# A GRU's candidate rows get a PSUM bank of their own, and the table stage keeps the transposed embedding

## The reference

```python
x = emb_table[input_ids]                       # (2048, 50, 128), a table of 12,501 rows
def step(h, xt):                               # 50 steps, h is (2048, 128)
    rec = h @ rec_kernel + b_r
    xz, xr, xh = jnp.split(xt, 3, axis=-1)
    rz, rr, rh = jnp.split(rec, 3, axis=-1)
    z = jax.nn.sigmoid(xz + rz)
    r = jax.nn.sigmoid(xr + rr)
    hh = jnp.tanh(xh + r * rh)
    return z * h + (1.0 - z) * hh
...
logits = last @ emb_table.T                    # (2048, 12501), fp32
```

## Time and profile before

| | |
|---|---|
| median of 3 runs | 1371.12 us (1370.25 to 1375.16) |
| the profiled execution's own time | 1370.22 us |
| its span, from the first to the last instruction | 1368.1 us |
| mean granted TensorE clock | 0.933 of 2.4 GHz |
| PE busy | 1180.8 us (86%) |
| PE's weight loads | 795.3 us (58%) |
| POOL busy | 784.2 us (57%) |
| DVE busy | 692.4 us (51%) |
| ACT busy | 686.6 us (50%) |
| DMA engines, mean | 215 GB/s |

### The profile page before, as it was taken

How to read it: one execution, slowest core, us unless ns; L and a number is a source line. 1 busy time by engine, 2 the same in 40 slices (tenths; PEclk the granted TensorE clock), 3 DMA queues, 4 the chain that set the end, 5 groups by cost and what they waited for, 6 DMA issues and landing times.

```text
span 1368.1 us, 16235 instructions
## 1 busy us (share of the span) xinstructions
PE 1180.8 (86%) x5590; PEld 795.3 (58%) x5590; DVE 692.4 (51%) x1191; ACT 686.6 (50%) x1203; POOL 784.2 (57%) x812
## 2 busy tenths in 40 slices
PE   7947778777878778778799999999999999999998
PEld 7933444343444334444466666666666668888776
DVE  7624455444545445445554555545555555444554
ACT  3522333333433333333456666666666667777644
POOL 0027667666776767667666666666666655555200
PEclk9979898888988888989999999999999999999999
DMA  8965555555555555555467887777887778888799
GB/s 292 366 179 153 142 152 146 147 152 141 154 146 148 146 154 146 148 143 159 132 196 239 260 254 253 250 238 253 256 261 253 237 249 269 285 282 284 239 365 333
DMA packets 127489, 294.21 MB, mean 215 GB/s; under 512 B 18096, under 2 KB 33456, under 8 KB 127408
## 3 DMA queue, kind: packets, MB, share of 16 engines
q0 software_dynamic: 51200, 157.34, 39.3%
q1 hardware_dynamic: 76208, 135.84, 29.6%
HBM read 171.30 MB, written 121.81 MB: 214 GB/s over the span
## 4 chain that ended last, share of the span: by engine, by line
PE 67%; another core or an unknown queue 11%; DVE 6%; ACT 6%; issue 5%; DMA 4%; POOL 0%; SPq 0%; DVEq 0%; ACTq 0%; POOLq 0%
PE r_ps L406 12%; PE c_ps L406 11%; PE z_ps L406 10%; PE x_ps L457 6%; PE x_ps L459 5%; PE x_ps L458 5%; PE c_ps L399 5%; PE r_ps L399 4%; PE z_ps L399 3%; DVE c_ps L765 2%; DMA gate_table<-gates 2%; ACT gates L562 2%; ACT gates L564 1%; DMA out_dram<-logits 1%
## 5 line engine op out<-in xcount | busy, mean ns | idle before, releaser
L335 POOL DMA_INDIRECT gathered<-gate_table,index x800 | 782.3, 978 | 495.9 <-issue 204.1
L564 ACT ACTIVATE gates<-z_ps,zr_bias 128x512 f32<-128x512 f32 (+1 forms) x250 | 151.6, 607 | 329.7 <-PE z_ps L406 162.7
L768 DVE TENSOR_TENSOR kept<-gates,state 128x512 f32<-128x512 f32 (+1 forms) x250 | 147.2, 589 | 237.5 <-ACT gates L564 192.0
L406 PE MATMUL r_ps<-state,w_rec_sb 128*128 128x512 f32 (+1 forms) x500 | 256.6, 598 | 0.0
L772 DVE SCALAR_TENSOR_TENSOR gates<-gates 128x512 f32<-128x512 f32 (+1 forms) x250 | 146.1, 585 | 209.0 <-issue 125.4
L399 PE MATMUL c_ps<-ident,gathered 128*128 128x128 f32 x800 | 116.4, 260 | 145.7 <-DVE c_ps L765 125.2
L406 PE MATMUL c_ps<-state,w_rec_sb 128*128 128x512 f32 (+1 forms) x500 | 235.1, 554 | 0.0
L406 PE MATMUL z_ps<-state,w_rec_sb 128*128 128x512 f32 (+1 forms) x500 | 233.8, 550 | 0.0
L399 PEld LDWEIGHTS c_ps<-ident,gathered 128*128 128x128 f32 x800 | 92.0, 144 | 232.6 <-DVE c_ps L765 180.7
L765 DVE SCALAR_TENSOR_TENSOR c_ps<-c_ps,bias_sb,gates 128x512 f32<-128x512 f32 (+1 forms) x250 | 162.0, 648 | 126.2 <-PE c_ps L406 47.2
L562 ACT ACTIVATE gates<-r_ps,zr_bias 128x512 f32<-128x512 f32 (+1 forms) x250 | 151.0, 604 | 143.3 <-PE r_ps L406 56.6
(11 more groups left out here) (78 smaller groups left out, 870.8 us busy)
## 6 DMA issues: line engine op xcount, KB each, us to landing
out_dram<-logits SPq DMA_DIRECT2D x192, 512.0 KB, 4.7
gate_table<-gates SPq DMA_DIRECT2D x24, 768.0 KB, 4.1
gathered<-gate_table,index POOLq DMA_INDIRECT x800
emb_rows<-in_L_rec_emb_table_dram SPq DMA_DIRECT2D x48, 256.0 KB, 4.6
out_dram<-logits SPq DMA_DIRECT2D x8, 213.0 KB, 3.9
logits<-in_r_input_ids_dram SPq DMA_DIRECT2D x1, 400.0 KB, 6.1
logits<-in_r_input_mask_dram SPq DMA_DIRECT2D x1, 400.0 KB, 6.5
gate_table<-gates SPq DMA_DIRECT2D x2, 192.0 KB, 9.2
```

Source lines behind the costliest of these rows:

```text
L335: nc.gpsimd.indirect_dma_start(gathered[:, q, n, :].bitcast(F32), None, table, bass.IndirectOffsetOnAxis(ap=index[:, g, n:n + 1], axis=0)) ...
L406: return nc.tensor.matmul(bank, w_rec_sb[:, gate * H:(gate + 1) * H], h, start=first, stop=True, skip_group_check=True)
L564: nc.scalar.activation(z_sb[:, b, 0:width], z_ps[:, b, 0:width], ACT.Sigmoid, bias=zr_bias[:, 0:1]).then_inc(s_z, 1)
```

## The change

Three things are changed together.

The candidate rows are turned into a bank pair of their own (x_ps), right behind the r rows. The state's candidate part stays alone in c_ps; DVE scales it into SBUF and adds the turned rows in a further instruction; ACT takes the tanh from SBUF. To make room, c_ps and z_ps have one bank each in place of two, and the logit units have a pair named u_ps. PE's matmul into c_ps now waits for the scaling of the block before, its z rows for the z sigmoid of the block before, its candidate rows for the addition two blocks before. A gather waits for `s_z_in` of the block four before.

`meanwhile` is now called ahead of the state's r matmul, behind both row groups, and `after` is gone: both logit units of a block stand there, whatever its width, and ACT copies both between its z sigmoid and its tanh.

The table stage splits the transposed chunks straight into embT_hi and embT_lo, which the logits use later, and the first stage's loads, transposes and copies of the vocabulary are gone. For this, `table_chunk` now gives partition p the rows p, 128 + p, 256 + p and 384 + p of a chunk. The projections use r_ps and x_ps in place of z_ps and r_ps; the last stage uses u_ps and r_ps.

```diff
-        z_sb, r_sb, cand = gates[:, 0], gates[:, 1], gates[:, 2]
+        z_sb, r_sb, pre = gates[:, 0], gates[:, 1], gates[:, 2]
-        rowsT_hi = state_hi[:, 2:4]
-        rowsT_lo = state_lo[:, 2:4]
...
-        z_ps = psum("z_ps", [P, SETS, BANK])
         r_ps = psum("r_ps", [P, SETS, BANK])
-        c_ps = psum("c_ps", [P, SETS, BANK])
-        x_ps = psum("x_ps", [P, 2, CHUNK])
+        x_ps = psum("x_ps", [P, SETS, BANK])
+        c_ps = psum("c_ps", [P, BANK])
+        z_ps = psum("z_ps", [P, BANK])
+        u_ps = psum("u_ps", [P, 2, CHUNK])
...
-            return rows[bass.ds(chunk * CHUNK, CHUNK), :].rearrange("(p n) h -> p n h", n=TPC)
+            return rows[bass.ds(chunk * CHUNK, CHUNK), :].rearrange("(n p) h -> p n h", p=P)
...
-            sp.wait_ge(s_rowsT_ps, FULL + 1)
-            for j, m in RAGGED:
-                sp.dma_start(emb_rows[0:m, 0, j, :], emb[ragged_rows(j, m), :]).then_inc(s_rows, 16)
-            for k in range(1, K2 - 1):
-                sp.wait_ge(s_rowsT, k)
-                sp.dma_start(emb_rows[:, 0], emb_chunk(k - 1)).then_inc(s_rows, 16)
...
-                    pool.wait_ge(s_turned, (k - 1) * QS + q + 1)
+                    pool.wait_ge(s_z_in, (k - 1) * QS + q + 1)
...
                 pe.wait_ge(s_gather[q], done)
-                pe.wait_ge(s_z, g + 1)
                 add_rows(r_bank, blk, q, 1, True)
+                if g >= SETS:
+                    pe.wait_ge(s_sum, g + 1 - SETS)
+                add_rows(x_bank, blk, q, 2, True)
+                if meanwhile is not None:
+                    meanwhile()
                 if started is not None:
                     pe.wait_ge(s_start, started)
                 if not start:
                     pe.wait_ge(s_state, g + 1 - SETS)
-                add_state(r_bank, h, 1, False).then_inc(s_rec, 1)
-                add_state(c_bank, h, 2, True).then_inc(s_rec, 1)
+                add_state(r_bank, h, 1, False).then_inc(s_r_in, 1)
+                if g > 0:
+                    pe.wait_ge(s_scaled, g)
+                add_state(c_bank, h, 2, True).then_inc(s_c_in, 1)
+                pe.wait_ge(s_z, g + SETS)
                 add_rows(z_bank, blk, q, 0, True)
                 add_state(z_bank, h, 0, False).then_inc(s_z_in, 1)
-                if meanwhile is not None:
-                    meanwhile()
-                pe.wait_ge(s_scaled, g + 1)
-                add_rows(c_bank, blk, q, 2, False).then_inc(s_turned, 1)
-                if after is not None:
-                    after()
...
-                if tiles_of(blk) == TPL:
-                    return (lambda: work((0,)), lambda: work((1,)))
-                return (lambda: work((0, 1)), None)
+                return lambda: work((0, 1))
...
-                act.wait_ge(s_rec, 2 * g + 1)
+                act.wait_ge(s_r_in, g + 1)
                 nc.scalar.activation(r_sb[:, b, 0:width], r_ps[:, b, 0:width], ACT.Sigmoid, bias=zr_bias[:, 1:2]).then_inc(s_r, 1)
                 act.wait_ge(s_z_in, g + 1)
-                nc.scalar.activation(z_sb[:, b, 0:width], z_ps[:, b, 0:width], ACT.Sigmoid, bias=zr_bias[:, 0:1]).then_inc(s_z, 1)
+                nc.scalar.activation(z_sb[:, b, 0:width], z_ps[:, 0:width], ACT.Sigmoid, bias=zr_bias[:, 0:1]).then_inc(s_z, 1)
                 if meanwhile is not None:
                     meanwhile()
-                act.wait_ge(s_turned, g + 1)
-                nc.scalar.activation(cand[:, b, 0:width], c_ps[:, b, 0:width], ACT.Tanh, bias=bias_sb[:, 0, 2:3]).then_inc(s_cand, 1)
-                if after is not None:
-                    after()
+                act.wait_ge(s_sum, g + 1)
+                nc.scalar.activation(pre[:, b, 0:width], pre[:, b, 0:width], ACT.Tanh, bias=bias_sb[:, 0, 2:3]).then_inc(s_cand, 1)
...
-                return (None, work) if tiles_of(blk) == TPL else (work, None)
+                return work
...
-                dve.wait_ge(s_rec, 2 * g + 2)
+                dve.wait_ge(s_c_in, g + 1)
                 dve.wait_ge(s_r, g + 1)
-                nc.vector.scalar_tensor_tensor(out=c_bank, in0=c_bank, scalar=bias_sb[:, 1, 2:3], in1=r,
+                nc.vector.scalar_tensor_tensor(out=new, in0=c_ps[:, 0:width], scalar=bias_sb[:, 1, 2:3], in1=r,
                                                op0=ALU.add, op1=ALU.mult).then_inc(s_scaled, 1)
+                dve.wait_ge(s_scaled, g + 1)
+                nc.vector.tensor_tensor(new, new, x, ALU.add).then_inc(s_sum, 1)
                 dve.wait_ge(s_z, g + 1 + SETS)
                 nc.vector.tensor_tensor(kept_b, z, h, ALU.mult).then_inc(s_kept, 1)
```

More of the change, by code:

```diff
@@ L181, in gru_logits @@
         s_scaled = sem("s_scaled")
+        s_sum = sem("s_sum")
         s_cand = sem("s_cand")
@@ L348, in turn_rows @@
                 for j, m in tiles:
-                    turned = nc.tensor.transpose(x_ps[:, bank, j * P:j * P + m], emb_rows[0:m, slot, j, :],
+                    turned = nc.tensor.transpose(u_ps[:, bank, j * P:j * P + m], emb_rows[0:m, slot, j, :],
                                                  ident[0:m, 0:m].bitcast(F32))
@@ L358, in transpose_rows, with project @@
                 turn_rows(s % 2, s, tiles).then_inc(s_rowsT_ps, 1)
-            def project(c, k, tiles=WHOLE, first=False):
+            def project(c, tiles=WHOLE, first=False):
                 pe.wait_ge(s_rowsT_lo, c + 1)
@@ L365, in project @@
                         pe.wait_ge((s_proj_dve, s_proj_act)[j % 2], c * (TPC // 2) + j // 2 - 1)
-                    bank = (z_ps, r_ps)[j // 2][0:m, j % 2, 0:G]
-                    high = rowsT_hi[:, k, j * P:j * P + m]
-                    low = rowsT_lo[:, k, j * P:j * P + m]
+                    bank = (r_ps, x_ps)[j // 2][0:m, j % 2, 0:G]
+                    high = embT_hi[:, c * CHUNK + j * P:c * CHUNK + j * P + m]
+                    low = embT_lo[:, c * CHUNK + j * P:c * CHUNK + j * P + m]
                     nc.tensor.matmul(bank, high, w_in_hi[:], start=True, stop=False)
@@ L375, in _ @@
             pe.wait_ge(s_w_in_parts, 2)
-            project(0, 0, first=True)
+            project(0, first=True)
             for s in range(1, SLOTS):
                 transpose_rows(s + 1, (s + 1) % SLOTS, 1 + (s + 1) // SLOTS)
-                project(s, s % 2)
+                project(s)
             for i in range(1, ROUNDS - 1):
@@ L407, in add_state, with step @@
                                         skip_group_check=True)
-            def step(k, q, blk, done, meanwhile=None, after=None, start=False, started=None):
+            def step(k, q, blk, done, meanwhile=None, start=False, started=None):
                 g = k * QS + q
@@ L414, in step @@
                 h = state[:, lane, c0:c0 + width]
-                z_bank, r_bank, c_bank = (t[:, q % SETS, 0:width] for t in (z_ps, r_ps, c_ps))
+                r_bank, x_bank = r_ps[:, q % SETS, 0:width], x_ps[:, q % SETS, 0:width]
+                c_bank, z_bank = c_ps[:, 0:width], z_ps[:, 0:width]
                 pe.wait_ge(s_gather[q], done)
-                pe.wait_ge(s_z, g + 1)
                 add_rows(r_bank, blk, q, 1, True)
+                if g >= SETS:
[3 more added lines that the diff above has]
+                    meanwhile()
                 if started is not None:
@@ L468, in work @@
                             pe.wait_ge(s_state_lo, parts)
-                        unit(tile + j, None if first else (k - K2) * QS + q, j, v0, width, x_ps[:, j])
-                if tiles_of(blk) == TPL:
-                    return (lambda: work((0,)), lambda: work((1,)))
-                return (lambda: work((0, 1)), None)
+                        unit(tile + j, None if first else (k - K2) * QS + q, j, v0, width, u_ps[:, j])
+                return lambda: work((0, 1))
             for q in range(QS):
-                step(0, q, FIRST[q], landed(0, 0, q), vocabulary(16 * len(RAGGED), None, RAGGED) if q == 0 else None,
-                     start=(q < SETS), started=2)
+                step(0, q, FIRST[q], landed(0, 0, q), start=(q < SETS), started=2)
             for k in range(1, K2):
                 for q in range(QS):
-                    step(k, q, FIRST[q], landed(0, k, q),
-                         vocabulary(16 * k + 16 * len(RAGGED), k, WHOLE) if q == 0 else None)
+                    step(k, q, FIRST[q], landed(0, k, q))
             for q in range(QS):
                 step(K2, q, SECOND[q], landed(K2, K2, q),
-                     *units(K2, q, SECOND[q], q * UPQ, FULL * CHUNK, REST, first=(q == 0), parts=1 + q // 2), started=4)
+                     units(K2, q, SECOND[q], q * UPQ, FULL * CHUNK, REST, first=(q == 0), parts=1 + q // 2), started=4)
             for i in range(1, K3 - K2):
@@ L518, in last_unit, with table_high @@
             tile = 3 * TPL + u % TPL
-            return ((x_ps, z_ps)[u % 4 // 2][:, u % 2], (u + UNITS3) % BUFFERS, nan_row[:, tile:tile + 1])
+            return ((u_ps, r_ps)[u % 4 // 2][:, u % 2], (u + UNITS3) % BUFFERS, nan_row[:, tile:tile + 1])
```

(6 more changed lines are left out.)

106 lines of the change are left out of this document (39 added, 67 removed).

## The result

The changed kernel takes 1498.3 us (median of 4 runs, 1497.2 to 1500.5) beside 1372.0 us before (1370.3 to 1375.2): a ratio of 1.092, 95% interval 1.0895 to 1.0944. The profiled execution has a span of 1496.6 us against 1368.1, 128.5 us more.

A forecast was written before the change was run, and what follows sets the result against it. It took POOL's issue as the first stage's floor and PE as the bound of the second and third; 1370.2 - 34 + 50 + 65 + 6 + 6 gave 1463 us, range 1420 to 1530.

The forecast's parts named there:

- +50: Third stage: logit units waiting for ACT's copies make each of 50 blocks 1.0 us longer, +50 us.
- +65: Second stage: the same wait for copies makes each of 50 block pairs 1.29 us longer, +65 us.
- the loop: Second and third stage: r to z, z sigmoid, first copy, two units, r again; 4.25 us at 256 columns, 5.91 at 512.
- rival 4: Second and third stage: copies are done in time and lengths stay; 1348 us, or 1314 with POOL's floor; chance 0.07.
- The 38 us held back in the second stage: Second stage: z sigmoids of 512 blocks starting late inside the loop, up to +38 us; taken as 0, kept for range.
- rival 3: Second and third stage: clock falls to 1.2 GHz; in half of the blocks +270 us, 1733 us; chance 0.06.
- the middle, -34: First stage: gain from removing PE's wait for scaling before the candidate rows, midway between 0 and -68 us.
- Its own low end: First stage: gain of 0, as late results stay and c and z have one bank each.
- rival 1: Late results don't shrink, so the first stage gains 0, or follow into the loop, second stage +38; 1535 us; chance 0.18.
- POOL's 515 us: First stage: POOL's gather issue sets a floor of about 515 us, 5.15 a block, limiting the gain to 68 us.
- the prediction's 3.4 each: Seams at blocks 100 and 200: units move ahead of r and wait for state_lo, 3.4 us each, +6 together.
- taken as 6, between 3 and 12: Table stage: loads and stores in smaller pieces run slower, +6 us, range 3 to 12.

The follow-up runs named there:

- copies first: Changed kernel with ACT copying a block's two logit units before that block's r sigmoid, not behind its z sigmoid: 1377.3 us, ratio to before 1.003.
- units behind z: Changed kernel with a block's logit units on PE moved behind its z matmul, ACT's order kept: 1367.9 us, one run.
- the table part alone: Kernel before with only the table-stage change: transposed embedding kept, later vocabulary transposes, copies and loads left out: 1375.6 us, ratio 1.0036.
- units behind z at the seams: Copies first, with logit units behind z and their copies behind the z sigmoid at blocks 100 and 200, lane 2's split later: 1384.4 us, ratio 0.9972.
- the kernel with the filler: Copies first, plus an unread 512-column full-precision matmul on PE behind each block 4 to 99: 1287.9 us on the second chip, 1395.3 on the third.

## Why the prediction was right, and where it was off

1. *The copies of the logits: right, term by term.* +50 was +47.9 for 47 blocks, 1.02 us each, and +65 was +63.9 for 48.5 pairs, 1.32 each against 1.29. Of the loop's parts, a sigmoid to the copy behind it took 0.37 (0.36 assumed), the copy to the unit 0.05. Moving the copies alone took 121 of the 126 us away again, and moving the units alone did as much, so rival 4's premise (copies in time) fails for exactly the reason given, ACT's order.
2. *The 38 us held back in the second stage: right to take 0.* In the changed kernel the late r, z and c of blocks 100 to 199 add up to 2.1 us. Before, z alone had 31.9. The prediction's reason (the loop leaves PE idle a fifth of the time) fits the other runs on that chip: with the loop open r, z and c add up to 15.9 us (copies first) and 84.5 us (units behind z) in these blocks. But such a sum is not a cost: the two take 428.5 and 431.5 us for 102 to 199.
3. *The clock: rival 3 didn't come.* With a stand of PE of 0.85 us in each block the granted clock was 0.99 and 1.00 in the two stages, the 2.4 GHz level: gaps of this size, one in 4.26 us, did not take the clock down. The Trainium skill (TensorE: Matmul & The Clock Gate, Why this matters for your kernels) warns of long idle gaps between bursts of matmuls. The trace agrees: around the stand of 6.32 us at the first seam the clock was 0.53 (684 to 695 us).
4. *The first stage: mis-sized, and this is most of the 35 us between 1463 and 1498.* Its step said that between 0 and -68 nothing decides, and took the middle, -34. It measured -2.6 (-9.9 on the third chip). Its own low end had a reason: late results sit on r, z and c alike. They did not shrink (191 us late before, 215 after), and the wait in PE's middle was a place where they were paid, not their source. It moved one matmul on: from 116.5 us ahead of the candidate rows to 79.3 ahead of the next block's c. The first half of rival 1 came true, the second did not. The sum also held POOL's 515 us fixed, and here they were not. POOL's waits did shrink, by 23.5 us in 98 to 681, two thirds of the 34 taken. What took this back is on POOL itself: on the first chip a gather of blocks 4 to 99 takes 1.00 us in the kernel before and in the one with the table part alone, and 1.04 to 1.05 in the three with DVE's addition; on the third chip 0.99 and 1.03 to 1.04. Over the 384 gathers that is 16.4 us on the first chip. The prediction had put DVE's addition at 0 beside POOL; that these 16 us are its price, and not that of another part of the change, isn't shown, and on the second chip kernels with the addition had 0.99 and 1.00. (The prediction's example of 8.6 us between PE and ACT holds other work of ACT until 457.74; ACT stood for 4.2 of them.)
5. *The seams: the unit's move was right, what comes with it was left out.* With the loop open, three blocks over a seam cost 16.3 - 12.9 = 3.4 and 14.8 - 11.4 = 3.4 us, the prediction's 3.4 each. The changed kernel paid +9.2 and +5.9. From the second, two blocks of the loop at 1.0 us take 2.0 and leave 3.9. The first also had r and z of block 99 late by 2.24 and 2.17 us, and a stretch at half clock from 684 to 695 us around the 6.32 us in which PE stood. On the third chip the same three blocks took 26.9 us, so this part moves from run to run.
6. *The table stage: +3.7, taken as 6, between 3 and 12.* Loads and stores in the small pieces do cost something. The hardware queue in 31 to 58 us moved 9.46 MB at a share of 105.3%, 333 GB/s at full share, against 366. That is a tenth less; the piece size of 512 B alone had been worth a fifth. In bytes moved in the same 27 us it is 9.46 against 9.91 MB, 4.5% less, since the share rose. The kernel with the table part alone started block 0 2.7 us later than before. That the piece size makes up all of it isn't shown. The Trainium skill (DMA: Bandwidth & Descriptors, Specifications) gives 512 B as the smallest transfer at line rate, by which the cost would have been 0. The trace disagrees: 333 GB/s against 366.

```profile
q1 hardware_dynamic: 9545, 9.46, 105.3%
```

*What stays open.* Why a result of PE reaches its reader late. PE's ends are modelled in the trace, so it can't even tell whether the matmul ran late or the word of it came late. It is not the gathers alone (the second chip gathers the same rows without it), and not PE's load alone (the first chip without gathers). Nor is PE's pause for a gather needed just before: in the kernel with the units behind z at the seams PE waits for none between blocks 26 and 39, and yet blocks 30 to 32, 37 and 38 have late results. Whether memsets in the gathers' place would bring it on a chip that has it wasn't seen, as that kernel ran on the second chip; nor was the changed kernel timed there. An estimate for that chip: 1496.6 less the 61 us between 575.2 and 513.8 is about 1435 us against the 1290.2 us that the kernel before spanned there, so the verdict would be the same and larger.

## What to carry to other kernels

Where a buffer with one consumer is refilled every round, walk the ring once in the consumer's program order: the copy that frees it, what stands ahead of that copy, and what that waits for. Here the ring closed through the z sigmoid and cost 1.0 us in every block, and moving the copy, not the buffer, opened it. A wait that is long because its input is late isn't gained by removing the wait: ask first whether the lateness has another reader. And run the kernel before beside every experiment, since one chip took 6% less than another here and made four theories look right at once. Last, a unit that sets the pace (POOL here) has a rate of its own that a change elsewhere may move; check its time per item, not only its waits.

## What the runs showed of the hardware

- The same kernel before took 1372, 1292 and 1387 us on three chips. The kernel with the filler shows where the difference lies, second chip against third: 517.0 and 583.0 us for blocks 0 to 99, 401.7 and 442.3 for 102 to 199, 150.9 and 150.8 for 202 to 249. The rate of gathers doesn't set the third stage apart: before, it is about 0.69, 0.67 and 0.62 a us in the three stages (four gathers in a block of 5.8 us, six in a pair of 8.9, two in a block of 3.24).
- Late results come in steps: those of c in the first stage of the changed kernel are 0.74, 1.44, 2.10 and 2.79 us late (two 0.5), many of z 2.17, 2.87, 4.26, 4.96, 5.63 and 7.05, near multiples of 0.71 us, and those of r up to 11.4. They mostly come in 2 or 3 blocks in a row, at most 5, and a stretch at half clock often follows the stand.
- With gathers but no late results PE waited for them 44.4 us in 450, and the clock stayed at 1.00 where it was 0.91 with late results, in the same kernel on the third chip:

```profile
120.00:570.00 450.00, 405.21 (x1710) 207.88 (x1708) 294.78 (x431) 170.48 (x258) 345.44 (x344) 1.00 0.53 151
```
